# A mixing loop that makes 12 of a tile's 32 slots itself instead of 16, with the closing norm done per four tiles

## The reference, cut to what matters

```
logits = (einsum('tzd,ed->tze', x, phi_w) + phi_b).reshape(t, z, n, p)   # n = 64 experts, p = 32 slots
D = softmax(logits, axis=3)                       # over the slots of an expert
C = softmax(logits, axis=2)                       # over the experts, for every slot
X_tilde = einsum('tznp,tzd->npd', D, x)           # slots gather tokens
...                                               # clip, norm, tanh, expert_w, expert_b
Y = einsum('tznp,npH->tzH', C, Y_tilde)           # tokens mix slots
x = layernorm(x + Y)
```

## Time and profile before

| what | value |
|---|---|
| median of 3 runs | 1399.61 us (1399.18 to 1403.23) |
| the profiled execution | 1401.92 us, of which the profile's span is 1399.90 us |
| busy share of the span | PE 92%, POOL 84%, DVE 79%, ACT 64% |
| `gather_slots` | ends at about 920 us of the span |
| `run_experts` | about 920 to 947 us |
| `mix_slots` | about 947 to 1399.9 us, a tile about every 7 us |
| DMA | 88 GB/s mean, queue q1 busy 26.4% of 16 engines |

### The profile page before, as it was taken

How to read it: one execution, slowest core, us unless ns; L and a number is a source line. 1 busy time by engine, 2 the same in 40 slices (tenths; PEclk the granted TensorE clock), 3 DMA queues, 4 the chain that set the end, 5 groups by cost and what they waited for, 6 DMA issues and landing times. The chain is left out here.

```text
span 1399.9 us, 31677 instructions
## 1 busy us (share of the span) xinstructions
PE 1293.0 (92%) x11006; PEld 1055.0 (75%) x11006; DVE 1109.3 (79%) x2462; ACT 896.6 (64%) x1670; POOL 1180.2 (84%) x1050
## 2 busy tenths in 40 slices
PE   4886789999999699999999999979999999999998
PEld 3664567777676477777777777748999999999997
DVE  4897456666666688888888888877999999999996
ACT  2897356666666476776776777735666666666664
POOL 7664568888888399999999999967999999999997
PEclk9998699999999999999999999999999999999999
DMA  5111243443443022222222222212222223232321
GB/s 167 47 40 55 84 134 117 121 122 115 125 121 94 24 84 89 92 83 91 91 84 90 91 87 87 84 48 94 84 88 83 88 84 89 82 91 80 92 79 31
DMA packets 83567, 123.61 MB, mean 88 GB/s; under 512 B 8593, under 2 KB 54226, under 8 KB 83410
## 3 DMA queue, kind: packets, MB, share of 16 engines
q1 hardware_dynamic: 81810, 117.16, 26.4%
q0 software_dynamic: 1088, 4.19, 1.0%
q10 hardware_dynamic: 512, 0.23, 0.1%
HBM read 70.28 MB, written 51.27 MB: 87 GB/s over the span
## 5 line engine op out<-in xcount | busy, mean ns | idle before, releaser
L997 POOL TENSOR_TENSOR gather_d<-gather_e,gather_rinv 128x1024 f32<-128x1024 f32 x128 | 244.8, 1913 | 36.6 <-DVE gather_rinv L976 36.5
L1256 POOL TENSOR_TENSOR mix_c<-mix_e,mix_rinv 128x1024 f32<-128x1024 f32 x128 | 240.9, 1902 | 18.7 <-DVE mix_rinv L1244 16.6
L1324 PEld LDWEIGHTS last_Y<-kept_phi,last_cT 128*128 128x128 f32 x2048 | 248.4, 192 | 7.3
L1324 PE MATMUL last_Y<-kept_phi,last_cT 128*128 128x128 f32 x2048 | 249.0, 275 | 0.0
L1340 ACT COPY last_cT<-last_T 128x1024 f32<-128x1024 f32 x128 | 128.4, 1003 | 132.1 <-PE last_T L1331 132.1
L822 POOL TENSOR_TENSOR cross_kd<-first_pack,kept_consts 128x624 fp32r<-128x624 f32 x128 | 155.6, 1237 | 63.7 <-DMA first_pack<-first_halves 54.1
L730 DVE TENSOR_REDUCE cross_mx<-cross_S 128x8 fp32r<-128x624 f32 x128 | 103.5, 809 | 113.0 <-PE cross_S L567 113.0
L1241 DVE TENSOR_REDUCE mix_sums<-mix_e 128x16 f32<-128x1024 f32 x128 | 155.8, 1217 | 34.4 <-ACT mix_e L1215 34.0
L972 DVE TENSOR_REDUCE gather_rsum<-gather_e 128x32 f32<-128x1024 f32 x128 | 156.1, 1220 | 25.9 <-ACT gather_e L945 25.9
L991 POOL TENSOR_TENSOR gather_dl<-gather_d,gather_dh 128x512 fp32r<-128x512 f32 x128 | 166.5, 1301 | 0.0
L934 ACT COPY gather_keep<-gather_L 128x256 f32<-128x256 f32 x256 | 94.7, 370 | 96.2 <-PE gather_L L908 95.9
(11 more groups left out here) (205 smaller groups left out, 3013.0 us busy)
## 6 DMA issues: line engine op xcount, KB each, us to landing
kept_logits<-gather_keep SPq DMA_DIRECT2D x128, 256.0 KB, 2.0
mix_read<-kept_logits SPq DMA_DIRECT2D x64, 512.0 KB, 3.7
first_halves<-first_qk SPq DMA_DIRECT2D x32, 412.0 KB, 3.0
first_pack<-first_halves SPq DMA_DIRECT2D x64, 128.0 KB
first_pack<-first_halves SPq DMA_DIRECT2D x32, 206.0 KB
first_pack<-first_halves SPq DMA_DIRECT2D x64, 78.0 KB
attn_xTg<-in_xT SPq DMA_DIRECT2D x16, 256.0 KB, 2.6
kept_xres<-in_x POOLq DMA_DIRECT2D x4, 1024.0 KB, 12.1
```

Source lines behind the costliest of these rows:

```text
L997: pool.tensor_tensor(dd[u % 4][:].rearrange("p i (n s) -> p i n s", n=16), e[u % 2][:], rinv[u % 2][:].rearrange("p (i n) -> p i n", i=2). ...
L1256: pool.tensor_tensor(self.cc[u % 2][:], self.e[u % 2][:], self.rinv[u % 2][:].unsqueeze(2).to_broadcast([128, 16, EXPERTS]), ALU.mult)\
L1324: ins = pe.matmul(psY[t % 2][:, 0:128], cT[u % 2][:, c, :], w.yk[:, 8 * (u % 2) + c, :], start=(u % 2 == 0 and c == 0), stop=(u % 2 == 1 a ...
```

## The change

MADE goes from 16 to 12. Mixing makes 12 slots (768 logits of a token) again and reads 20 (1280). The halves that are summed, divided and turned stay at 16 slots, so half 0 now consists of 12 made and 4 read slots: its exponentials are two instructions, and the second of them needs read logits that POOL has lowered. `lower` becomes two instructions, first the 4 read slots of half 0, then the 16 of half 1. The read buffers are two instead of three and larger.

The closing norm is done for four tiles at once: sum and power on POOL over four columns, the shift on DVE, and one store of 512 rows instead of one of 256 for every two tiles. The residual buffers hold four tiles and are three deep; ACT's scaling stays one instruction per tile and runs with lag 16 instead of 8. The diff, cut to that:

```
-MADE = SLOTS // 2
+MADE = 12
...
-    READS = 3
+    READS = 2
...
-        reach(sync, self.less_ready, t - self.READS + 1)
+        reach(sync, self.less_ready, 2 * (t - self.READS + 1))
...
-            for i in range(2):
-                ins = pe.matmul(self.psL[t % 2][:, i, :], xs[:, at], ws[:, 512 * i:512 * i + 512],
-                                start=n == 0, stop=n == 2)
+            for i, c in enumerate((slice(0, 512), slice(512, MADE * EXPERTS))):
+                ins = pe.matmul(self.psL[t % 2][:, i, 0:c.stop - c.start], xs[:, at], ws[:, c], start=n == 0, stop=n == 2)
...
     def exponentials(self, act, t, half):
         reach(act, self.c_ready, 2 * t - 1 + half)
+        less, e = self.less[t % 2], self.e[half]
         if half == 0:
             act.wait_ge(self.shifted, t + 1)
             act.wait_ge(self.lowered, t + 1)
-            act.activation(self.e[0][:].rearrange("t p n -> t (p n)"),
-                           self.psL[t % 2].rearrange("t i x -> t (i x)"), ACT.Exp).then_inc(self.e_ready, 1)
+            act.activation(e[:, 0:MADE, :].rearrange("t p n -> t (p n)"), self.made(t), ACT.Exp)
+            act.wait_ge(self.less_ready, 2 * t + 1)
+            act.activation(e[:, MADE:16, :].rearrange("t p (i n) -> t i p n", i=2), less[:, :, 0:16 - MADE, :], ACT.Exp)\
+                .then_inc(self.e_ready, 1)
         else:
-            act.wait_ge(self.less_ready, t + 1)
-            act.activation(self.e[1][:].rearrange("t p (i n) -> t i p n", i=2), self.less[t % 2][:], ACT.Exp)\
+            act.wait_ge(self.less_ready, 2 * t + 2)
+            act.activation(e[:].rearrange("t p (i n) -> t i p n", i=2), less[:, :, 16 - MADE:SLOTS - MADE, :], ACT.Exp)\
                 .then_inc(self.e_ready, 1)
...
     def lower(self, pool, t):
         pool.wait_ge(self.high_ready, t + 1)
         reach(pool, self.e_ready, 2 * t - 2)
-        pool.tensor_tensor(self.less[t % 2][:], self.read[t % self.READS][:],
-                           self.high[t % 2][:].unsqueeze(1).unsqueeze(3).to_broadcast([128, 2, 16, 32]),
-                           ALU.subtract).then_inc(self.less_ready, 1)
+        for p in (slice(0, 16 - MADE), slice(16 - MADE, SLOTS - MADE)):
+            pool.tensor_tensor(self.less[t % 2][:, :, p, :], self.read[t % self.READS][:, :, p, :],
+                               self.high[t % 2][:, p].unsqueeze(1).unsqueeze(3).to_broadcast([128, 2, p.stop - p.start, 32]),
+                               ALU.subtract).then_inc(self.less_ready, 1)
...
-                for t in tiles(k, 8):
-                    act.wait_ge(shift_ready, t + 1)
...
+                for t in tiles(k, 16):
+                    p, i = t // 4, t % 4
+                    if i == 0:
+                        act.wait_ge(shift_ready, p + 1)
+                        reach(act, stored[p % 2], 16 * (p // 2))
...
+                for p in fours(k, 9):
+                    dve.wait_ge(rstd_ready, p + 1)
+                    dve.scalar_tensor_tensor(out=shift[p % 3][:], in0=mv[p % 3][:, :, 0], scalar=-1.0, in1=rstd[p % 3][:],
+                                             op0=ALU.mult, op1=ALU.mult).then_inc(shift_ready, 1)
...
-                for t in tiles(k, 7):
-                    pool.wait_ge(mv_ready, t + 1)
-                    pool.tensor_tensor(veps[:], mv[t % 2][:, 1:2], w.eps[:, 0:1], ALU.add).then_inc(ve_done, 1)
-                    pool.wait_ge(ve_done, t + 1)
-                    reach(pool, res_ready, t - 1)
-                    pool.tensor_tensor(rstd[t % 2][:], veps[:], w.neg_half[:, 0:1], ALU.pow).then_inc(rstd_ready, 1)
-                    pool.wait_ge(rstd_ready, t + 1)
-                    pool.tensor_scalar(shift[t % 2][:], mv[t % 2][:, 0:1], -1.0, rstd[t % 2][:], ALU.mult, ALU.mult)\
-                        .then_inc(shift_ready, 1)
+                for p in fours(k, 7):
+                    pool.wait_ge(mv_ready, 4 * p + 4)
+                    pool.tensor_tensor(veps[:], mv[p % 3][:, :, 1], w.eps[:, 0:4], ALU.add).then_inc(ve_done, 1)
+                    pool.wait_ge(ve_done, p + 1)
+                    reach(pool, res_ready, 4 * (p - 2))
+                    pool.tensor_tensor(rstd[p % 3][:], veps[:], w.neg_half[:, 0:4], ALU.pow).then_inc(rstd_ready, 1)
```

More of the change, by code:

```diff
@@ L1174, in __init__ @@
         self.w = w
[L1175 to L1178, removed]
+        self.read = [st.sb(f"read{i}", [128, 2, SLOTS - MADE, 32]) for i in range(self.READS)]
+        self.high = [st.sb(f"high{i}", [128, SLOTS - MADE]) for i in range(2)]
+        self.less = [st.sb(f"less{i}", [128, 2, SLOTS - MADE, 32]) for i in range(2)]
+        self.mx = [st.sb(f"mx{i}", [128, MADE], F32R) for i in range(2)]
         self.e = [st.sb(f"e{i}", [128, 16, EXPERTS]) for i in range(2)]
@@ L1214, in exponentials, with made @@
             act.wait_ge(self.lowered, t + 1)
-            act.activation(self.e[0][:].rearrange("t p n -> t (p n)"),
-                           self.psL[t % 2].rearrange("t i x -> t (i x)"), ACT.Exp).then_inc(self.e_ready, 1)
-        else:
-            act.wait_ge(self.less_ready, t + 1)
-            act.activation(self.e[1][:].rearrange("t p (i n) -> t i p n", i=2), self.less[t % 2][:], ACT.Exp)\
+            act.activation(e[:, 0:MADE, :].rearrange("t p n -> t (p n)"), self.made(t), ACT.Exp)
+            act.wait_ge(self.less_ready, 2 * t + 1)
+            act.activation(e[:, MADE:16, :].rearrange("t p (i n) -> t i p n", i=2), less[:, :, 0:16 - MADE, :], ACT.Exp)\
+                .then_inc(self.e_ready, 1)
+        else:
+            act.wait_ge(self.less_ready, 2 * t + 2)
+            act.activation(e[:].rearrange("t p (i n) -> t i p n", i=2), less[:, :, 16 - MADE:SLOTS - MADE, :], ACT.Exp)\
                 .then_inc(self.e_ready, 1)
+    def made(self, t):
+        return self.psL[t % 2].rearrange("t i x -> t (i x)")[:, 0:MADE * EXPERTS]
     def peaks(self, dve, t):
@@ L1226, in peaks @@
         reach(dve, self.lowered, t - 1)
-        dve.tensor_reduce(mx[:].rearrange("t (i p) -> t i p", i=2),
-                          self.psL[t % 2].rearrange("t i (p n) -> t i p n", p=8), X, ALU.max).then_inc(self.mx_ready, 1)
+        dve.tensor_reduce(mx[:], self.made(t).rearrange("t (p n) -> t p n", n=EXPERTS), X, ALU.max)\
+            .then_inc(self.mx_ready, 1)
         dve.wait_ge(self.loaded[t % self.READS], 16 * (t // self.READS + 1))
-        reach(dve, self.less_ready, t - 1)
+        reach(dve, self.less_ready, 2 * t - 2)
         dve.tensor_reduce(self.high[t % 2][:], self.read[t % self.READS][:].rearrange("t i p n -> t p i n"),
@@ L1234, in peaks @@
         dve.wait_ge(self.mx_ready, t + 1)
-        second = self.psL[t % 2][:, 1, :].rearrange("t (p n) -> t p n", p=8)
-        dve.tensor_tensor(second, second, mx[:, 8:16].bitcast(F32).unsqueeze(2).to_broadcast([128, 8, EXPERTS]),
+        second = self.made(t)[:, 512:MADE * EXPERTS].rearrange("t (p n) -> t p n", n=EXPERTS)
+        dve.tensor_tensor(second, second, mx[:, 8:MADE].bitcast(F32).unsqueeze(2).to_broadcast([128, MADE - 8, EXPERTS]),
                           ALU.subtract).then_inc(self.lowered, 1)
@@ L1269, in mix_slots @@
         cT = [st.sb(f"cT{i}", [128, 8, 128]) for i in range(2)]
-        y = [st.sb(f"y{i}", [128, 128]) for i in range(2)]
+        y = [st.sb(f"y{i}", [128, 4, 128]) for i in range(3)]
         stats = st.sb("stats", [128, 6])
[L1272 to L1276, removed]
+        mv = [st.sb(f"mv{i}", [128, 4, 2]) for i in range(3)]
+        veps = st.sb("veps", [128, 4])
+        rstd = [st.sb(f"rstd{i}", [128, 4]) for i in range(3)]
+        shift = [st.sb(f"shift{i}", [128, 4]) for i in range(3)]
+        res = [st.sb(f"res{i}", [128, 4, 128]) for i in range(2)]
         psT = st.ps("T", [128, 8, 128])
@@ L1292, in tiles, with fours @@
             return [(k - lag) // 2] if (k - lag) % 2 == 0 and 0 <= k - lag < UNITS else []
-        ORDER = range(UNITS + 9)
+        def fours(k, lag):
+            return [t // 4 for t in tiles(k, lag) if t % 4 == 3]
+        ORDER = range(UNITS + 15)
         @block.sync
         def _(sync):
-            for t in range(TILES + 4):
-                if t + READS - 1 < TILES:
+            for t in range(TILES + 12):
+                if EARLY <= t + READS - 1 < TILES:
                     mix.load(sync, t + READS - 1)
[L1301 to L1304, removed]
+                if t >= 12 and t % 4 == 0:
+                    p = (t - 12) // 4
+                    sync.wait_ge(res_ready, 4 * p + 4)
+                    sync.dma_start(out[p * 512:(p + 1) * 512, :].rearrange("(b s) d -> s b d", b=4), res[p % 2][:])\
                         .then_inc(stored[p % 2], 16)
             for i in range(2):
-                sync.wait_ge(stored[i], 16 * (TILES // 4))
+                sync.wait_ge(stored[i], 16 * (TILES // 8))
         @block.tensor
@@ L1344, in _ @@
                         mix.exponentials(act, t, 1)
-                for t in tiles(k, 8):
-                    act.wait_ge(shift_ready, t + 1)
```

(4 more changed lines are left out.)

9 lines of the change are left out of this document (5 added, 4 removed).

## The result

The changed kernel takes 1428.67 us (median of 4 runs, 1427.03 to 1430.69). In the same series of runs the kernel before takes 1399.39 (median of 4). The ratio is 1.0206, 95% interval 1.0183 to 1.0229: the change costs 2.1%. The forecast was 1435, range 1418 to 1452.

A forecast was written before the change was run, and what follows sets the result against it. A closed dependence chain from lowering to lowering (6.89 of 6.96 us) was taken as the bound. 1401.92 + 32 (chain) + 2 (norm) + 1.5 (tail) = 1437.4 us profiled, hence median 1435, range 1418 to 1452.

The forecast's parts named there:

- The bound: Mixing loop: a closed chain from one tile's lowering to the next, 6.89 us of a 6.96 us tile, decides its length.
- Rival A: Mixing loop: relief of the full engines decides, a tile falls to PE's 6.58 us, -23 us, 1377; chance 0.07.
- The chain's three pieces: Lowering-to-lowering chain: short lowering +0.58, largest made logit -0.24, largest read logit +0.27 us; new chain 7.50, +32 us.
- The low bound: Short lowering on POOL: a quarter of the long one's 1.914 less the overlap, 0.44 us; chain 7.33.
- the high one: Short lowering on POOL, priced by rows with two full operands: 0.91 us after the overlap; chain 7.86.
- The new wait: Half 0's second exponential on ACT waits for the short lowering; costs the chain nothing, first division waits 0.7 us.
- The second wait: POOL waits again for the reciprocal before each tile's second division, about 0.2 us.
- PE's idle time: Mixing loop: PE, needing 6.58 us per tile, would be idle for about 0.9 us of a tile.
- Norm of four: POOL's norm after the lowerings in one tile of four: 0 to 0.35 us, 15 times; taken as 2 us.
- Gathering: ACT's copies of 320 instead of 256 logits, 256 times, hidden by waits for PE: taken as 0.
- Tail: End of the kernel: four scalings behind the last norm and a longer power: +1.5 us, from 0 to 3.
- Loads: Mixing's two read buffers: 640 KB land in 4.6 us, asked for 11 us ahead; no cost.

The follow-up runs named there:

- e3: The changed kernel with the 256-element short lowering done once more, ahead of the two lowerings: 1467.91 us, ratio 1.0489 to the kernel before.
- e4: The changed kernel with the same extra short lowering behind the two lowerings, ahead of the divisions: 1440.11 us, ratio 1.0281 to the kernel before.
- e5: The changed kernel with DVE taking the next tile's largest read logit a tile earlier: 1418.64 us, ratio 1.0129 to the kernel before.
- e6: On top of e5, 12 made slots, POOL lowers the next tile ahead of this tile's divisions: 1401.92 us, ratio 1.0020 to the kernel before.
- e8: On e6, ACT makes all exponentials before copying the turned half, and PE's order follows: 1379.43 us, ratio 0.9857 to the kernel before.
- e1: The kernel before, 16 made slots, with only norm, scaling and stores going by four tiles: 1412.83 us, ratio 1.0097.

## Why the prediction was right

*The bound.* That a chain of dependences sets the tile, though PE was at 100.00 and POOL at 94.67, held. e3 and e4 show it by place, e5 and e6 by taking pieces out. Rival A, by which the relief of the full engines decides, is refuted for this change: the relief was used up by waits, and it came back only in e8, once the loops no longer held the tile. The Trainium skill, "Perfetto Trace Analysis", section on the most-contended engine, has the engine of the highest occupancy optimised first; here the work taken off the two busiest engines made the kernel 2.1% slower, and it paid only in e8, where no loop was longer than PE's own work.

*The chain's three pieces.* Forecast +0.58, -0.24 and +0.27. Measured from start to start: lowerings to exponential 2.58 against 2.00, +0.58; the made maximum 0.81 against 1.08, -0.27; the read maximum 1.55 (1.48 and the hand-over) where 1.21 + 0.08 was counted, +0.26. New chain 7.46 against the 7.50, +30.75 us over 60 tiles against +32. The low bound (a quarter of a long lowering) and the high one (two full operands) are both excluded by the 0.61 of the short lowering; the line through the broadcast row gave 0.62. The rate of the Trainium skill ("GPSIMD Engine Reference", section on elementwise cycle accounting) gives an estimate of 2.2 for the long one. The trace does not agree: after the change the long lowering still takes 1.92.

*The new wait.* ACT's second exponential stays off the chain: half 1's exponential starts 2.58 after the lowerings, as worked out. The first division was put at 3.2 after the lowerings with 0.7 of waiting: 3.12 and 0.62. The second wait was put at about 0.2 and the room ahead of the next lowering at 0.37: 0.24 and 0.30.

*PE's idle time* was put at 0.9 per tile, 7.5 less 6.58. The rows show 7.3% of 7.475, 0.55. The need of 6.58 was right, as e8's 6.60 shows; the busy time is not the need, since PE's records fill more of a longer tile (92.68% of 7.475 is 6.93).

*Norm of four*: forecast 2 us, measured nothing. After it, POOL goes through both divisions without a wait and the next lowering starts on time, 7.47 after the last:

```profile
1075.65 1.01 POOL L1406 TENSOR_TENSOR last_rstd<-last_veps,kept_neg_half 128x4 f32<-128x4 f32 x1
1076.63 3.77 POOL L1262 TENSOR_TENSOR mix_c<-mix_e,mix_rinv 128x1024 f32<-128x1024 f32 x2
1080.39 2.49 POOL L1255 TENSOR_TENSOR mix_less<-mix_read,mix_high 128x256 f32<-128x256 f32 x2
...
1080.56 0.46 DVE L1374 SCALAR_TENSOR_TENSOR last_shift<-last_mv,last_rstd 128x4 f32<-128x4 f32 x1
```

The power of four costs 1.01, the lower of the two rows. DVE's shift falls beside the short lowering, which holds it for only 0.46, and DVE had that to spare. That the shift is harmless was right by luck: e1 shows it at 1.50 and on the path.

*Gathering*: no change, right. The copies got longer and PE still stands in front of them, 95.3 us where it was 96.2:

```profile
L934 ACT COPY gather_keep<-gather_L 128x320 f32<-128x320 f32 x256 | 108.7, 425 | 95.3 <-PE gather_L L908 95.0
```

*Tail*: forecast +1.5, measured +1.2. The last rows answer to the earlier trace rows: four scalings, 0.4 each, behind the shift.

```profile
1423.81 0.16 DVE L1374 SCALAR_TENSOR_TENSOR last_shift<-last_mv,last_rstd 128x4 f32<-128x4 f32 x1 [1.40 <-POOL last_rstd L1406]
1424.01 1.65 ACT L1360 ACTIVATE last_res<-last_y,last_shift,last_rstd 128x128 f32<-128x128 f32 x4 [3.84 <-DVE last_shift L1374]
```

*Loads*: the 640 KB were put at 4.6 us in proportion and harmless. They land in 3.9, and nothing in the changed kernel's loop waits for them (answer to the earlier trace rows).

```profile
mix_read<-kept_logits SPq DMA_DIRECT2D x64, 640.0 KB, 3.9
```

*What is missing in the sum* is the 3.45 us that the part ahead of tile 3 is shorter. The first matmul of gathering starts at 475.95 instead of 477.60, so 1.65 of it lies in stages that the change doesn't touch. Such shifts are scatter between executions: in the traces of e1 and e3, whose stages up to there are the same, gathering starts at 472.88 and at 478.72. One profiled execution of each kernel can't tell more about the rest. The sum forecast for the profiled execution was 1437.4: with 3.3 less in the loop and the norm, 0.3 in the tail and 3.45 ahead of them it is the 1430.3 measured.

## What to carry to other kernels

Before taking work off a full engine, walk one period of the timeline from an instruction to its next occurrence: if a path through several engines closes with less slack than the relief, only what stands on this path counts, and a piece added to it costs its whole length (here 0.57 us for an instruction of 0.61). Opening one loop shows the next (7.46, then 6.74, then PE's 6.59), and a move that breaks one loop can close a longer one (8.19). Here the order on PE, ACT, DVE and POOL was moved together, and with that the change that by itself lost 2.1% gained 1.4%.

## What the runs showed of the hardware

The shift is DVE's one instruction in this loop with two operands in SBUF, and it lasts until the POOL instruction in flight is done. At 128x4 it takes 0.16 us with POOL idle (the last one of the changed kernel), 0.46 beside a short lowering, 0.91 beside the end of a division, 1.50 and 1.89 beside a long lowering; each time it ends within 0.02 us of the POOL instruction. Other instructions with two such operands were not tried. The Trainium skill, "Trainium Architecture — The Big Picture", section on what this means for kernel authors, calls the port pair that the two engines share an exclusive lock and not a split of bandwidth. The runs agree, with these numbers. DVE's sum, with its one operand in SBUF, keeps its length beside POOL: at 128x1024 it lasts 1.16 to 1.22 throughout the traces before and after.
